# A decoder layer on one core: transfers from three queues, self maxima by groups, preparation behind the self loop, six tiles normalised on ScalarE

## The reference, cut to what matters

```python
# x (16, 56, 128); ctx (16, 1500, 128); bias (16, 1500); 16 heads of 8; all float32
x = x + self_attention(layernorm(x), qkv_w, qkv_b, proj_w, proj_b)      # softmax over 56 keys
x = x + cross_attention(layernorm(x), ctx, bias, Wq, Wk, Wv, Wo)        # softmax over 1500 keys, bias per key
x = x + moe(layernorm(x), Wg, W1, W2, W3, Ws1, Ws2, Ws3)                # softmax gate, top 4 of 32, SwiGLU 128->64->128
```

## Time and profile before

| | |
|---|---|
| median of 3 runs | 511.76 us (511.7 to 512.29) |
| the profiled execution, its own time | 511.28 us |
| span of the profiled execution | 509.5 us |
| mean granted TensorE clock | 0.924 |
| busy: PE, DVE, ACT, POOL | 437.9, 365.4, 324.7, 270.7 us |
| first self round on TensorE | 32.17 us |
| self loop, first scores to last transposition | 43.46 to 80.4 us |
| scores of batch 0 in the cross loop | 118.97 us |
| scores of batch 1 | 137.30 us |

### The profile page before, as it was taken

The page is one execution under the profiler, slowest core; times in us unless marked ns, Lnnn a source line. Parts: engine busy times, 40 slices in busy tenths (PEclk is TensorE's granted clock), DMA queues, the critical chain, the costliest instruction groups (busy, mean ns, idle before and its releaser), DMA issues.

```text
span 509.5 us, 16014 instructions
## 1 busy us (share of the span) xinstructions
PE 437.9 (86%) x6736; PEld 288.8 (57%) x6736; DVE 365.4 (72%) x561; ACT 324.7 (64%) x670; POOL 270.7 (53%) x211
## 2 busy tenths in 40 slices
PE   2328974279999999999999999999989986899995
PEld 1125753135667667667667767767766763344442
DVE  7335334877777777777777777777778345899995
ACT  6232640026888888888888888888866773355553
POOL 8845783336856856856856856851422310254430
PEclk9855996578999999999999999999999896999997
DMA  6290757119897587677687578573202020012101
GB/s 166 80 222 5 79 156 159 61 48 227 192 150 163 149 136 163 152 132 169 146 133 166 150 132 141 115 72 100 92 12 63 19 50 0 17 46 49 31 1 36
DMA packets 77966, 53.26 MB, mean 105 GB/s; under 512 B 62472, under 2 KB 69192, under 8 KB 77896
## 3 DMA queue, kind: packets, MB, share of 16 engines
q1 hardware_dynamic: 76568, 51.25, 46.8%
q10 hardware_dynamic: 816, 0.98, 0.7%
q0 software_dynamic: 512, 0.03, 0.1%
HBM read 17.05 MB, written 0.46 MB: 34 GB/s over the span
## 4 chain that ended last, share of the span: by engine, by line
PE 63%; DVE 15%; issue 8%; ACT 4%; DMA 4%; POOL 2%; ACTq 2%; SPq 1%; DVEq 0%; POOLq 0%
PE ps L968 18%; PE ps L821 11%; PE ps L944 6%; DVE mx L1528 4%; DVE v L1626 3%; PE ps L824 3%; PE ps L367 3%; ACT v L1309 3%; PE ps L368 3%; PE ps L369 3%; DVE xn L1351 3%; PE ps L749 2%; PE ps L752 2%; PE ps L750 2%; PE ps L854 2%
## 5 line engine op out<-in xcount | busy, mean ns | idle before, releaser
L1528 DVE TENSOR_REDUCE mx<-ps 120x2 f32<-120x1000 f32 x192 | 221.2, 1195 | 63.1 <-PE ps L944 63.0
L1250 ACT ACTIVATE p<-ps 125x448 f32<-125x448 f32 x288 | 140.2, 544 | 10.6 <-PE ps L968 7.6
L968 PE MATMUL ps<-qall,ks 128*125 128x224 f16 x768 | 130.3, 275 | 3.6 <-ACT p L1250 1.8
L612 POOL TENSOR_TENSOR k<-k,zero 128x500 f16<-128x500 f32 x48 | 48.9, 1018 | 106.9 <-ACT k L1184 101.5
L968 PEld LDWEIGHTS ps<-qall,ks 128*125 128x125 f16 x768 | 75.2, 137 | 41.2 <-ACT p L1250 21.5
L821 PE MATMUL ps<-p,v 125*27 125x168 f32 x1152 | 64.7, 311 | 0.1
L616 POOL TENSOR_TENSOR k<-k 128x500 f16<-128x500 f32 x48 | 55.2, 1151 | 3.8
L944 PE MATMUL ps<-ks,qall 31*56 31x500 f16 x768 | 44.4, 401 | 14.3 <-DVE mx L1528 14.2
L1250 ACT ACTIVATE wnat<-ps 125x448 f32<-125x448 f32 x96 | 47.0, 541 | 6.0 <-PE ps L968 6.0
L599 POOL TENSOR_TENSOR ch<-ctx,ch 128x1536 f16<-128x1536 f32 x16 | 49.8, 3113 | 1.3
L589 POOL TENSOR_TENSOR ch<-ctx,zero 128x1536 f16<-128x1536 f32 x16 | 44.0, 2747 | 9.0 <-issue 7.6
(11 more groups left out here) (176 smaller groups left out, 782.6 us busy)
## 6 DMA issues: line engine op xcount, KB each, us to landing
ks<-k SPq DMA_DIRECT2D x48, 375.0 KB
ctx<-in_ctx SPq DMA_DIRECT2D x16, 672.0 KB
ks<-in_L_ffn_W SPq DMA_DIRECT2D x48, 64.0 KB, 2.0
ks<-brow SPq DMA_DIRECT2D x32, 46.9 KB
ctx<-in_ctx SPq DMA_DIRECT2D x16, 78.0 KB
ks<-k ACTq DMA_DIRECT2D x3, 224.0 KB, 4.0
qall<-q SPq DMA_DIRECT2D x12, 49.0 KB
ct<-ch SPq DMA_TRANSPOSE x32, 6.3
```

What stands on the lines that cost most here:

```text
L612: nc.gpsimd.tensor_tensor(k12[:, 0, cols], k32[:, cols], zero[:].rearrange("p a b -> p (a b)").to_broadcast([128, CH]), ALU.add).then_inc( ...
L968: last = mm(stb[score_bank(r, c, s, half)][0:KP, 224 * (g % 2):224 * (g % 2) + 224], ks[c % 3][:, g, KP * s:KP * s + KP], qall[:, g, :, 3 ...
L1250: A(p[s % 4][0:KP, 448 * half:448 * half + 448], stb[score_bank(r, c, s, half)][0:KP, 0:448], ACT.Exp, scale=SCALE).then_inc(exp_done, 1)
L1528: V.tensor_reduce(mx[:, h:h + 2, k // 2], mxb[0:120, 2 * pair:2 * pair + 2, 0:CH], axis=AX.X, op=ALU.max).then_inc(mx_read, 1)
```

## The change

Transfers. The self stacks are issued from three queues: SyncE takes query row 0 and key rows 0 and 2, GpSimd query row 1, ScalarE query row 2 and key row 1. SyncE then waits for the first self round (mself_psum) before it loads context 1 and transposes context 0. The cross query rows of batches 0 and 1 go from SyncE (row 0, half of row 2) and GpSimd (row 1, the other half) and none from ScalarE. GpSimd zeroes the second half of qall only after VectorE has written all normalised tiles (xn_ok).

Maxima. Self rounds run first over all batches of the even groups, then of the odd ones. A turn of the maxima is two matmuls of 64 columns in place of 16 of 8, and the scores of step 0 wait for both sets of row 127.

Preparation. PREP keeps the keys of batch 0 in steps 1 to 3. The values of batch 0 and the keys of batch 1 move behind the self loop, into misc: keys between the three maximum rounds, values after the transposes and ahead of the query projection. OUT_STEP is 4, and turn and query projection of tile 0 are both in step 6.

Normalisation. VectorE writes nbias = -mean * rstd (one instruction) and ScalarE applies scale and bias to six tiles, after the first piece of keys and before the second. GpSimd's constants for the experts move behind its batch loop, and `rstd_of(1, 1)` ahead of the key split of batch 1.

Left out below: declarations of tiles and semaphores, changed indices in the counting helpers, and the renaming of m // 2, m % 2.

```diff
-PREP = {1: (0, "K0"), 2: (0, "K1"), 3: (0, "K2"), 4: (0, "V0"), 5: (0, "V1"), 6: (0, "V2"),
-        7: (1, "K0"), 8: (1, "K1"), 9: (1, "K2")}
+PREP = {1: (0, "K0"), 2: (0, "K1"), 3: (0, "K2")}
...
-OUT_STEP, TURN_STEP, Q_STEP = 5, 7, 8
+OUT_STEP, Q_STEP = 4, 6
...
 BEFORE_LOOP = 2 * PAIRS
-FIRST = {"K": 2, "V": 1}
+FIRST = {"K": 1, "V": 0}
...
-        def query_rows(engine, n, k, row, part, done):
+        def query_rows(engine, n, k, row, part, done, heads_of=range(HG)):
...
-            for j in range(HG):
+            for j in heads_of:
...
             sp.wait_ge(q1_ok, 2)
-            for row in range(2):
-                query_rows(sp, 0, 0, row, 0, qs_ok[0])
+            query_rows(sp, 0, 0, 0, 0, qs_ok[0])
+            sp.wait_ge(kself1_ok, 2)
+            sp.wait_ge(kfill_ok, 1)
+            for row in (0, 2):
+                sp.dma_start(ks[2][row::4, :, 0:T], k12[:, 0, 0:T]).then_inc(kself_in[0], 16)
+            sp.wait_ge(mself_psum, 1)
...
             sp.wait_ge(q1_ok, 3)
-            for row in range(2):
-                query_rows(sp, 1, 0, row, 0, qx_ok[0][0])
+            query_rows(sp, 1, 0, 0, 0, qx_ok[0][0])
+            sp.wait_ge(q2_ok, 3)
+            query_rows(sp, 1, 0, 2, 1, qx_ok[0][0], (0, 1))
...
                     else:
-                        pool.wait_ge(kself_in, 3 * 16)
+                        pool.wait_ge(kself_in[0], 2 * 16)
+                        pool.wait_ge(kself_in[1], 16)
...
             pool.wait_ge(rstd_ok, 2)
+            pool.wait_ge(xn_ok, TT)
...
+            pool.wait_ge(q1_ok, 2)
+            query_rows(pool, 0, 0, 1, 0, qs_ok[1])
...
                 split_keys(0, j)
-            memset(ones_h[:], 1.0)
-            memset(before[:], 1.0)
-            memset(pairsel[:], 0.0).then_inc(pairsel_step, 1)
-            nc.gpsimd.iota(expert_no[:], pattern=[[1, NE]], base=0, channel_multiplier=0,
-                           allow_small_or_imprecise_dtypes=True)
-            pool.wait_ge(pairsel_step, 1)
-            select(out=before[:], in_=before[:], compare_op=ALU.is_gt, fill=0.0, base=0,
-                   pattern=[[1, 128]], channel_multiplier=-1)
...
+            pool.wait_ge(st_done, 1)
+            pool.wait_ge(q1_ok, 3)
+            query_rows(pool, 1, 0, 1, 0, qx_ok[0][1])
+            pool.wait_ge(q2_ok, 3)
+            query_rows(pool, 1, 0, 2, 1, qx_ok[0][1], (2, 3))
+            rstd_of(1, 1)
...
-            rstd_of(1, 1)
...
+            memset(ones_h[:], 1.0)
+            memset(before[:], 1.0)
+            memset(pairsel[:], 0.0).then_inc(pairsel_step, 1)
+            nc.gpsimd.iota(expert_no[:], pattern=[[1, NE]], base=0, channel_multiplier=0,
+                           allow_small_or_imprecise_dtypes=True)
+            pool.wait_ge(pairsel_step, 1)
+            select(out=before[:], in_=before[:], compare_op=ALU.is_gt, fill=0.0, base=0,
+                   pattern=[[1, 128]], channel_multiplier=-1)
...
                             g = odd + 2 * upper
-                            last = mm(ps[64 * upper:64 * upper + S, 4 * odd + j, S * k:S * k + S],
+                            last = mm(ps[64 * upper:64 * upper + S, 4 * (m % 2) + j, S * k:S * k + S],
...
-            def self_max_rows(half):
...
-                pe.wait_ge(mself_ok, 4 * half + 4)
+            def self_max_rows(odd):
...
+                pe.wait_ge(mself_ok, 4 * odd + 4)
...
-                    for b in range(8):
-                        last = mm(ps[0:8, (4, 2)[half] + upper, S * b:S * b + S],
-                                  mself[rows, half, :, :, b].rearrange("p g j -> p (g j)"),
-                                  ident[rows, rows], start=True, stop=True)
+                    last = mm(ps[0:64, (4, 2)[odd] + upper, 0:S], mself[rows, odd].rearrange("p j b -> p (j b)"),
+                              ident[rows, rows], start=True, stop=True)
...
-            pe.wait_ge(qs_ok[0], 2 * HG * 16)
-            pe.wait_ge(qs_ok[1], HG * 16)
-            pe.wait_ge(kself_in, 3 * 16)
+            for n in range(3):
+                pe.wait_ge(qs_ok[n], HG * 16)
+            pe.wait_ge(kself_in[0], 2 * 16)
+            pe.wait_ge(kself_in[1], 16)
...
+            self_max_rows(1)
...
                 if s < PAIRS:
-                    pe.wait_ge(mself_row[s // 4], 2 * 16)
...
-                        pe.wait_ge(mself_ok, 7)
+                        pe.wait_ge(mself_row[0], 2 * 16)
+                        pe.wait_ge(mself_row[1], 2 * 16)
...
-                    if s == 0:
-                        self_max_rows(1)
-                    else:
+                    if s:
...
                     last.then_inc(vself_psum, 1)
+                if s == Q_STEP:
+                    pe.wait_ge(chain_read, 1)
+                    transpose_norm(1, 0, 3, chain_psum)
...
                     out_project(0, 0, chain_bank, chain_psum)
-                if s == TURN_STEP:
-                    pe.wait_ge(chain_read, 1)
-                    transpose_norm(1, 0, 3, chain_psum)
...
                 if k == 0:
-                    pe.wait_ge(qx_ok[part_of(b)][0], 2 * HG * 16)
-                    pe.wait_ge(qx_ok[part_of(b)][1], HG * 16)
+                    pe.wait_ge(qx_ok[part_of(b)][0], (3 * HG if part_of(b) else 6) * 16)
+                    if part_of(b) == 0:
+                        pe.wait_ge(qx_ok[0][1], 6 * 16)
...
             for k in range(ROUNDS // 2):
+                large_use(0, -2, f"K{k}")
...
+            for k in range(ROUNDS // 2):
+                large_use(0, -2, f"V{k}")
...
             act.wait_ge(qzero_ok, 2)
-            query_rows(act, 0, 0, 2, 1, qs_ok[1])
+            query_rows(act, 0, 0, 2, 1, qs_ok[2])
...
-            for row, part in ((0, 0), (1, 1), (2, 0)):
-                act.dma_start(ks[2][row::4, :, 0:T], k12[:, part, 0:T]).then_inc(kself_in, 16)
+            act.dma_start(ks[2][1::4, :, 0:T], k12[:, 1, 0:T]).then_inc(kself_in[1], 16)
...
-            def self_max_rows(half):
...
-                act.wait_ge(mselft_psum, half + 1)
-                bank = (4, 2)[half]
-                A(mrow_self[:, half], ps[0:8, bank:bank + 2, 0:HALF], ACT.Copy, scale=1.0 / BIG).then_inc(mselfr_ok, 1)
-                act.wait_ge(mselfr_ok, half + 1)
+            def self_max_rows(odd):
...
+                act.wait_ge(mselft_psum, odd + 1)
+                bank = (4, 2)[odd]
+                A(mrow_self[:, odd], ps[0:64, bank:bank + 2, 0:S], ACT.Copy, scale=1.0 / BIG).then_inc(mselfr_ok, 1)
+                act.wait_ge(mselfr_ok, odd + 1)
...
-                    act.dma_start(qall[MAXROW:MAXROW + 1, 2 * upper:2 * upper + 2, :, 8 * half:8 * half + 8]
-                                  .rearrange("o g h b q -> o (g h) (b q)"), mrow_self[:, half, upper]
-                                  ).then_inc(mself_row[half], 16)
+                    g = odd + 2 * upper
+                    act.dma_start(qall[MAXROW:MAXROW + 1, g].rearrange("o h b q -> o (h b q)"), mrow_self[:, odd, upper]
+                                  ).then_inc(mself_row[odd], 16)
...
                       scale=SCALE).then_inc(exp_done, 1)
-                if s == 0:
-                    self_max_rows(1)
...
                       ps[:, 6:8, 0:224].rearrange("p u (k q) -> p u k q", k=4), ACT.Copy).then_inc(o_read, 1)
-                if s == TURN_STEP:
+                if s == Q_STEP:
...
-                if s == Q_STEP:
...
-                    act.wait_ge(q2_ok, 3)
-                    query_rows(act, 1, 0, 2, 1, qx_ok[0][1])
...
+            self_max_rows(1)
...
+            take_keys(0, 1, 0)
+            act.wait_ge(nbias_ok, 1)
+            for j in range(*LN_TILES[1][1]):
+                A(xn[:, j], xs[:, j], ACT.Identity, bias=nbias[:, j:j + 1], scale=rstd[:, j:j + 1]).then_inc(xn_ok, 1)
+            for j in (1, 2):
+                take_keys(0, 1, j)
...
+            for j in range(3):
+                take_values(0, 0, j)
...
                     norm_apply(1, 0)
-                if s == TURN_STEP:
+                if s == Q_STEP:
...
-                if s == Q_STEP:
...
-            take_round(0, -2, 2, 0)
-            norm_apply(1, 1)
-            for k in range(1, ROUNDS // 2):
+            dve.wait_ge(rstd_ok, 4)
+            tiles = slice(*LN_TILES[1][1])
+            V.scalar_tensor_tensor(nbias[:, tiles], mv[:, tiles, 0], -1.0, rstd[:, tiles], ALU.mult, ALU.mult
+                                   ).then_inc(nbias_ok, 1)
+            for k in range(ROUNDS // 2):
```

More of the change, by code:

```diff
@@ L101, in uses_before @@
     i = 3 * r + c if isinstance(r, int) else c
-    n = BEFORE_LOOP + sum(used(0, j, u) for j in range(-1, i) for u in MISC)
+    n = BEFORE_LOOP + sum(used(0, j, u) for j in range(-2, i) for u in MISC)
     return n if isinstance(r, int) else n + 3 * len(MISC) * r
@@ L108, in misc_index @@
     i = 3 * r + c if isinstance(r, int) else c
-    return uses_before(r, c) + [u for u in MISC if used(0, i, u)].index(use)
```

(23 more changed lines are left out.)

## The result

The changed kernel takes 505.07 us (median of 4 runs, 503.67 to 505.75), against 511.73 us for the kernel before (4 runs, 511.45 to 512.29): a ratio of 0.9865, 95% interval 0.9842 to 0.9888. It is faster by 6.7 us where I had forecast 13.3, and the time lies 0.6 above 504.5, the upper end of my wider range (the forecast's own range was 495 to 501). The profiled execution of after took 503.67 us with a span of 501.9; it is the fastest of the four.

A forecast was written before the change was run, and what follows sets the result against it. With no engine full, the chain up to batch 1's scores was taken as the bound, collected at q1's end. Terms 7.3 - 1.0 + 5.7 + 1.3 = 13.3 took 511.28 to 498.0, median 498.5; range 495 to 501, wider 491.5 to 504.5.

The forecast's parts named there:

- The stacks: Before the self loop: rows issued from three queues bring the first self round to 24.9, 7.3 us earlier, normalisation included.
- the early normalisation: At the start: zeroing held until xn is written saves 2.4 us, counted inside the 7.3 to the first self round.
- nbias at 1.0: Behind the self loop: VectorE's nbias instruction, held by GpSimd's key split, is charged 1.0 us.
- The maxima: First self round to first scores: 13.0 us instead of 11.3; with the lower clock this part loses 1.0.
- the self loop without preparation: Self steps 4 to 10 without moved pieces: 18.1 us instead of 23.84, a gain of 5.7.
- a step without a piece takes 2.42: Self loop: step 4's 3.21 us less the values piece's 0.79, as no engine but TensorE is full.
- That is 18.1: Self loop: the stated sum in us of the forecast times of steps 4 to 10, before 23.84.
- TensorE stays at 1.2 GHz in the self loop: Rival, self loop: less work keeps the clock low, steps take about 4.5 us, 515 in all; chance 0.04.
- busy nearly all of a step: Self loop: argument against the low-clock rival, that TensorE stays this busy even without a piece.
- Preparation comes back in full: Rival, self loop and behind: gain 5.7 becomes 3.5 and 1.3 becomes -1.5; 503.5 us, chance 0.12.
- the term behind the loop: Output projection to q1: statistics unchanged, then 16.4 us instead of 17.7, a gain of 1.3.
- the end of q1 starts the chain to batch 1: Before the batch loop: q1's end starts SyncE's query issues and an unchanged 32.8 us chain to batch 1's scores.

The follow-up runs named there:

- e7: e10 with the turn of tile 0 (step 6) parted from its cross query projection (step 7): 496.99 us, ratio 0.9699.
- e5: The changed kernel with GpSimd's split of context 2 held until VectorE has normalised tile 0: 499.68 us, ratio 0.9763.
- e10: e9 with all nine preparation pieces kept in self steps 1 to 9: 500.10 us, ratio 0.9763.
- e9: The changed kernel with GpSimd's splits waiting both for tile 0's scaling and for nbias: 501.96 us, ratio 0.9788.
- e6: The changed kernel with the second and third value piece of batch 0 behind the query projection: 504.12 us, ratio 0.9844.
- e8: The kernel before with only the normalisation part (nbias on VectorE, six tiles on ScalarE, maximum rounds in succession): 510.19 us, ratio 0.9956.
- e2: The changed kernel with all nine preparation pieces back in self steps 1 to 9: 499.41 us, ratio 0.9764.
- e11: e7 with idle matmuls in TensorE's waits from the output projection to the end of iteration 0: 493.52 us, ratio 0.9636.

## Why the prediction was right and wrong

**Right.** The stacks and the early normalisation: 7.3 forecast, 7.55 measured, and the last row was ScalarE's key row at 3.10 (4.0 forecast). The direction. nbias at 1.0 (0.98), which the Trainium skill had suggested ("SBUF — State Buffer", section "Who interferes with whom"); e7's 0.17 shows that the hold was the cause. SyncE's twelve issues and the steady iteration are as they were.

**The maxima.** From the first round to the first scores it is 14.16 instead of 11.3, where I had 13.0. I had taken the shortest landing of the row, 1.6, and not that the context traffic moved out of the stacks' way would be in flight beside it; the four of the change took 2.6 to 5.0. By step 4 the stage has lost 1.8 (7.55 - 5.79) where I had 1.0, and step 4 starts 0.5 later than forecast.

**The step that failed is the self loop without preparation**, "a step without a piece takes 2.42" and "That is 18.1". It took 21.85, so the 5.7 became 2.0; this is 3.7 of the 5.4 us that are missing when SyncE issues the queries (13.3 forecast, 7.9 measured). A slip stands in it as well: the step times listed add up to 18.4, and by the terms the output projection belonged at 68.7 and not at 67 to 68.

The sum took the piece's 0.79 out of a step as if TensorE alone set its length, and at the high clock. In the change steps 4 and 5 took 2.94 and 2.64 instead of 2.8 and 2.4, step 6 came out at 4.46 instead of 3.9, and steps 7 to 10 at 11.81 instead of 9.3. Of these 2.5, 1.7 is the clock: in e5 the same steps, with the same waits, take 10.12 with the clock falling between 66 and 68 instead of 62 and 64. I had allowed 0.4 for it. The rest is with the waits for tok and attn, 0.74 and 0.20 to 0.35 each. Like for like (e10 to e9, one profile of each) six pieces fewer shorten steps 4 to 10 by 1.3 and not by six times 0.79. The three gone from steps 4 to 6 bring 1.7 of their 2.4. The three gone from steps 7 to 9 bring nothing: 10.20 becomes 10.60, with the wait of 0.74 for tok as before and the clock falling between 66 and 68 instead of 70 and 72.

The rival "TensorE stays at 1.2 GHz in the self loop" had the mechanism and too large a dose: it came in the last four steps and not from the start. What I had held against it, that TensorE stays "busy nearly all of a step", was not so (4.39 of 6.00 us). Nearest to the time was "Preparation comes back in full" (503.5): it gave the loop 3.5 and the term behind it -1.5, where 2.0 and 0.1 were measured. It had the loop's part by evictions on ScalarE and not by the clock; behind the loop it had the lower clock and the waits for ScalarE, as they came (0.69 ahead of the second and third value piece).

**The second is the term behind the loop**: forecast to the query issue 16.4, measured 17.65, and nothing gained. The transposes came when I had said (7.4 after the statistics; 7.9 forecast). Then the value pieces took 2.24 each at the low clock, two of them in full view, where I had taken at most 1.95.

**A premise fell too**: that the end of q1 starts the chain to batch 1, and that this chain keeps its 32.8. It took 34.0 in the change. The chain of the kernel before runs into batch 1 through SyncE's keys, GpSimd's split and its send of the maxima; in the profile of the change it runs through VectorE's maxima and then TensorE. In e6 the end of q1 came 5.6 earlier, and batch 1 0.3 earlier, though there the later landing of the maxima takes part of it. In the other profiles the query issue and batch 0 kept a distance of 13.9 to 14.8 us (15.9 in e8). My reading is that both hang on the same TensorE queue, VectorE's maxima among it, and that the one doesn't start the other; that is argued from the chains. By batch 1 6.6 of the 7.9 are left, and the whole profiled execution is 7.6 shorter; where the 1.0 comes back in the batch loop is open.

**What stood behind the missing time.** Two things bring time back. First, ordering tile 0's scaling ahead of GpSimd's split of context 2 brings 5.4 (e5). Keeping the preparation brings as much (e2), and both together, with nbias freed, no more (e10), so these two are not separate losses. That e5 works by ending the hold is not shown: in the profiled run of the change the scaling wasn't held either, and yet it is 4.0 slower than that of e5 (503.67 and 499.67), with the clock as the difference up to the output projection. How often the hold comes in the change no run tells. The likely reading is that e5 and e2 act on how long TensorE waits around step 6, and so on the clock afterwards; that is argued.

Second, the low clock from the loop's end to iteration 0: filling the waits brings 3.5 (e11 against e7). It stays open why the clock fell after 62 in the change's profile and after 66 in e5's, which run alike up to there. The profiles show for a rise that its moment differs by itself: e10 and e9 run the same code up to step 3, and the granted clock reaches 1.00 at 44 in the one and between 46 and 47 in the other, the scores of step 2 taking 0.57 and 0.95. The rule of the Trainium skill on the clock ("TensorE: Matmul & The Clock Gate", section "Part 1: The HAM clock gate") says that the moment at which the clock rises varies from run to run of one kernel, and the traces agree. For the fall no run here isolates it.

## What to carry to other kernels

Work taken out of an engine's queue shortens a step only by what no other chain fills: follow the producer of each wait once without the piece before subtracting it, and ask what the clock was there with the piece in place. Short independent pieces in the waits of a latency chain can cost far less there than elsewhere: six of them cost the self loop 1.3 us (e10 against e9), and a value piece behind it 2.24 by itself. Where a long GpSimd instruction can start just ahead of a short VectorE one, as here (0.34 us alone, up to 2.45 held), order the short one first by a semaphore, and where a transfer is moved out of one row's way, look for the next small row that it will meet.

## What the hardware showed that I had not expected

A single VectorE scaling of 128x128 with one tensor input took 0.34, 1.09, 1.12, 1.29, 1.95 or 2.45 us, by when GpSimd's split began; where it took longer than 0.34 it ended within 0.1 us of the split's end. The Trainium skill says ("SBUF — State Buffer", section "Who interferes with whom") that the order of issue decides who is held, and the traces agree: 0.34 ahead of the split in e5.

The mean clock over the span does not rank executions. The kernel before ran at 0.917 in 511.39 us and at 0.945 in 512.42. One reason can be read in the front: the change's profile has a granted clock of 1.00 from 20 to 46, and the scores of steps 0 and 2 take 0.95 us in it, just as in e9's, which has 0.50 there. In such a stretch the durations of equal instructions tell the pace, and the recorded clock doesn't; at 62 to 72 the two agree.

Idle matmuls paid for themselves: 3.5 us from 86 of 128x384 (the trace has 82), most of them standing where TensorE waited anyway.
